# Banded attention: weights applied to the normalized rows first, value matrices a batch at a time

## The reference

```python
xq = _rms_norm(x @ wq, q_norm_w, EPS); xk = _rms_norm(x @ wk, k_norm_w, EPS); xv = x @ wv   # 8 heads of 128
bias = slopes[:, None, None] * rel             # rel = key position - query position
invalid = (rel > 0) | (rel < -WINDOW)          # a query sees itself and the 16 tokens before it
bias = jnp.where(invalid[None, :, :], NEG, bias)
probs = jax.nn.softmax(einsum('bhqd,bhkd->bhqk', q, k) * scale + bias[None], axis=-1)
y = einsum('bhqk,bhkd->bhqd', probs, v)        # then heads side by side
return y @ wo
```

## Time and profile before

| | us |
|---|---|
| runs, median of 3 | 1302.38 (1298.53 to 1306.37) |
| profiled execution | 1303.17 |
| its span | 1301.3 |
| banded attention on TensorE, first dM to last out1 | 972.17 to 1139.81 |
| TensorE busy, share of the span | 89% |
| VectorE | 70% |
| ScalarE | 67% |
| GpSimd | 48% |

### The profile page before, as it was taken

The page is one execution under the profiler, slowest core; times in us unless marked ns, Lnnn a source line. Parts: engine busy times, 40 slices in busy tenths (PEclk is TensorE's granted clock), DMA queues, the critical chain, the costliest instruction groups (busy, mean ns, idle before and its releaser), DMA issues.

```text
span 1301.3 us, 17124 instructions
## 1 busy us (share of the span) xinstructions
PE 1161.3 (89%) x6126; PEld 614.8 (47%) x6126; DVE 914.4 (70%) x1753; ACT 876.4 (67%) x1130; POOL 618.7 (48%) x455
## 2 busy tenths in 40 slices
PE   5899999999999999987888888999989999976865
PEld 2444444444444444422222222677766777733444
DVE  5666667766776677568989896255547777678885
ACT  2799999999989998963777777445545665633411
POOL 3577777777767776884555551033320000044232
PEclk8999999999999999986999999899999999978778
DMA  7100000000000000100000000000010000000000
GB/s 188 50 1 1 1 1 1 1 1 1 1 0 1 1 1 1 65 1 17 2 1 1 2 1 2 1 1 1 1 61 1 1 1 1 1 1 1 0 9 25
DMA packets 25631, 14.48 MB, mean 11 GB/s; under 512 B 14558, under 2 KB 24396, under 8 KB 25420
## 3 DMA queue, kind: packets, MB, share of 16 engines
q1 hardware_dynamic: 25548, 13.39, 3.7%
HBM read 12.34 MB, written 1.05 MB: 10 GB/s over the span
## 4 chain that ended last, share of the span: by engine, by line
PE 36%; POOL 30%; issue 19%; DVE 13%; ACT 1%; POOLq 0%; DMA 0%; SPq 0%; ACTq 0%; DVEq 0%
DVE ARENA L1048 6%; POOL ARENA L2466 6%; POOL ARENA L2464 6%; POOL ARENA L2460 6%; PE PS L914 4%; PE PS L889 4%; POOL WQ L2477 3%; POOL ARENA L2490 3%; PE PS L803 3%; PE PS L1269 3%; PE PS L1258 2%; PE PS L1253 2%; PE PS L1245 2%; PE PS L770 2%; PE PS L754 2%
## 5 line engine op out<-in xcount | busy, mean ns | idle before, releaser
L2320 DVE TENSOR_SCALAR ARENA<-PS,ARENA 128x512 f32<-128x512 f32 x256 | 174.6, 744 | 67.8 <-PE PS L1954 67.3
L1048 DVE TENSOR_REDUCE ARENA<-PS 128x1 f32<-128x512 f32 x256 | 161.1, 683 | 27.2 <-PE PS L770 26.6
L959 ACT ACTIVATE ARENA<-PS 128x1024 f32<-128x1024 f32 x128 | 128.8, 1026 | 58.3 <-PE PS L789 58.0
L2133 ACT ACTIVATE ARENA<-ARENA 128x2048 f32<-128x2048 f32 x64 | 122.2, 1911 | 62.3 <-DVE ARENA L2320 61.8
L1954 PE MATMUL PS<-ARENA 64*128 64x512 f32 x512 | 130.9, 631 | 0.0
L2140 ACT ACTIVATE ARENA<-ARENA,consts_sb 128x2048 f32<-128x2048 f32 x64 | 124.6, 1994 | 0.4
L1964 PE MATMUL PS<-ARENA 128*64 128x512 f32 x512 | 118.7, 606 | 1.3 <-issue 1.3
L2146 ACT ACTIVATE ARENA<-ARENA 128x2048 f32<-128x2048 f32 x64 | 118.3, 1897 | 0.0
L1204 POOL TENSOR_TENSOR ARENA<-ARENA 128x512 f32<-128x512 f32 x32 | 40.6, 1270 | 142.0 <-DVE ARENA L1162 141.9
L2473 POOL TENSOR_SCALAR WQ<-ARENA,consts_sb 128x512 bf16<-128x512 f32 x32 | 22.3, 695 | 159.8 <-DVE ARENA L2296 159.8
L770 PE MATMUL PS<-ARENA 32*128 32x512 bf16 x256 | 74.3, 405 | 25.7 <-DVE ARENA L1048 21.4
(11 more groups left out here) (279 smaller groups left out, 2693.6 us busy)
## 6 DMA issues: line engine op xcount, KB each, us to landing
ARENA<-in_window_bias_dram SPq DMA_DIRECT2D x1, 1536.0 KB, 6.8
WKVG<-in_L_attn_W_in_dram SPq DMA_DIRECT2D x3, 448.0 KB, 5.5
X<-in_x_dram SPq DMA_DIRECT2D x4, 256.0 KB, 4.4
W<-in_L_ffn_w_dram SPq DMA_DIRECT2D x1, 1024.0 KB
out_dram<-X SPq DMA_DIRECT2D x4, 256.0 KB, 2.3
BV<-in_L_attn_b_in_dram SPq DMA_DIRECT2D x1, 512.0 KB, 6.1
Wout<-in_L_attn_W_out_dram SPq DMA_DIRECT2D x1, 512.0 KB, 4.8
WQ<-in_L_attn_wq_dram SPq DMA_DIRECT2D x1, 512.0 KB, 3.3
```

Of the source, the lines that this page charges most:

```text
L959: act.activation(PT[m % PT_SLOTS], bank(("cP", m)), ACT.Exp, scale=0.5).then_inc(sem("c_exp"), 1)
L1048: dve.tensor_reduce(NMX[:, w % 2, t, h:h + 1], bank(("cS", n, j)), AX.X, ALU.max, negate=True).then_inc(sem("c_max"), 1)
L2133: act.activation(chunk(u, half), chunk(u, half), ACT.Sqrt).then_inc(sem("rooted"), 1)
L2320: dve.tensor_scalar(D[:, u % 2, kt, hd, :], bank(("S", u, c)), K2[:, u % 2, kt, hd:hd + 1], 1e-30, ALU.add, ALU.max).then_inc(sem("guarded ...
```

## The change

The product (band weights) x (rows) x (`NVO1` part) is made from the other side. The value matrices are gone. `finish(n)` now multiplies the tile's 128 keys as normalized rows, one stationary tile, with the turned weights of four heads at a time, two products of 4 x nq columns (dZ, two banks). ScalarE copies the first four heads' half and VectorE the second into `ZT`, which holds a batch. Only then, for a whole batch and in two parts (`project_out`: columns 0 to 351 once tile 2 is done, 352 to 511 once tile 4 is done), each head's part of `NVO1` is multiplied with its `ZT` columns and summed over the heads in dO. The key rows of tiles 0 and 4 lie in `Y` as they are; those of tiles 1 to 3 are turned back from `XT` once per batch (`turn_keys`, dX, three transposes) and copied by ScalarE to `KTOK`. VectorE's copy of the values goes. Out1 and the addition to the stream come one step later, and the turned next layernorm comes behind dT.

```diff
@@ -344,8 +344,19 @@
 
 def turned_out_batch(n):
 
-    b, ti = divmod(n - 1, len(TILES1))
+    b, ti = divmod(n - 2, len(TILES1))
     return b - 1 if ti == 0 and 1 <= b < B else None
+
+
+PARTS1 = ((0, 352, 3), (352, 512, 5))
+
+
+def projected(n):
+
+    b, ti = divmod(n, len(TILES1))
+    if ti == 4:
+        return b, 0
+    return (b - 1, 1) if ti == 1 and b else None
 
 
 def stage_d_jobs():
...
@@ -361,11 +372,11 @@
                 out += [(("dM", b, h), 1, [(("d_q", "d_k")[h % 2], HD1 // 2 * b + h // 2 + 1)], "D")]
             if b + 1 < B:
                 out += [(("yt", b + 1, m), 1, [("xqk", 2 * (b + 1) + m + 1)], "D") for m in range(2)]
-        return out + [(("dS", n), 2, [("d_biased", n + 1)], "D"), (("dV", n), 2, [("d_v", n + 1)], "D")]
+            out += [(("dX", b), 1, [("d_keys", b + 1)], "DO")]
+        return out + [(("dS", n), 2, [("d_biased", n + 1)], "D")]
 
     def finish(n):
-        b, ti = divmod(n, len(TILES1))
-        return [(("dO", b), 1, [("d_ot", b + 1)], "DO")] if ti == 0 else []
+        return [(("dZ", n), 2, [("d_z_low", n + 1), ("d_z_high", n + 1)], "D")]
 
     def turn_out(b):
         return [(("out1", b), 1, [("x_new", 3 * B + b + 1)], "D")]
...
@@ -374,13 +385,15 @@
     for n in range(steps):
         if n + 2 < steps:
             jobs += start(n + 2)
+        if projected(n) is not None and projected(n)[1] == 0:
+            jobs += [(("dO", projected(n)[0]), 1, [("d_ot", projected(n)[0] + 1)], "DO")]
         if turned_out_batch(n) is not None:
             jobs += turn_out(turned_out_batch(n))
         if n:
             jobs += finish(n - 1)
+        jobs += [(("dT", n), 2, [("d_pt", n + 1)], "D")]
         if n >= 9 and (n - 4) % len(TILES1) == 0:
             jobs += ln_job(4, n // len(TILES1) - 1, "D")
-        jobs += [(("dT", n), 2, [("d_pt", n + 1)], "D")]
     return jobs + finish(steps - 1) + turn_out(B - 1)
 
 
...
@@ -649,7 +662,9 @@
         WD = Wout[:, 0:3, :]
         QT1, at = carve(0, [HD1, S])
         OT1, at = carve(at, [S])
-        V1, at = carve(at, [4, HD1 * P])
+        KTOK, _ = carve(at, [2, 3, P])
+        at += 4 * HD1 * P
+        ZT, _ = carve(20480, [2, HD1, S])
         SM, at = carve(at, [3, HD1, P])
         PT1, at = carve(at, [2, HD1, P])
         XQK, at = carve(at, [2, 2, S])
...
@@ -702,8 +717,8 @@
         HQT, at = carve(at, [2, 2, 3 * P])
 
         for name in ("d_weights_in", "bias_in", "e_weights_in", "gram_turned", "gram", "zy", "ss", "r_log",
-                     "r_rms", "ym", "xqk", "d_q", "d_k", "d_biased", "d_v", "d_max", "d_exp", "d_norm", "d_pt",
-                     "d_ot", "d_summed", "folded_weights", "folded_values", "folded_scores", "e_k", "e_v4", "e_vx", "e_kx", "e_ctx4", "e_q", "e_biased", "e_shift", "e_max",
+                     "r_rms", "ym", "xqk", "d_q", "d_k", "d_biased", "d_keys", "d_z_low", "d_z_high", "d_max", "d_exp", "d_norm", "d_pt",
+                     "d_ot", "folded_weights", "folded_values", "folded_scores", "e_k", "e_v4", "e_vx", "e_kx", "e_ctx4", "e_q", "e_biased", "e_shift", "e_max",
                      "f_rounded", "f_added", "e_exp", "e_rc", "e_p", "e_pt", "e_o", "xb4", "mask_bias",
                      "f_weights_in", "f_wq", "f_w", "f_yq", "f_x", "f_silu", "f_h", "f_hq", "f_ht", "x_final"):
             sem(name)
...
@@ -1211,7 +1226,7 @@
 
         def turn_next(n):
 
-            return stats_next(n - 3)
+            return stats_next(n - 2)
         SCALE1 = float(P ** -0.5)
 
         def norms(pe, begin, done, b):
...
@@ -1232,6 +1247,14 @@
                     for t in range(QT):
                         mm = pe.transpose(o[:, t * P:(t + 1) * P], YM[:, m, t, :], ident)
                     done(mm, ("yt", b, m))
+
+            def turn_keys(b):
+                pe.wait_ge(sem("xt_ready"), norm_no(3, b))
+                o = begin(("dX", b))
+                for i in range(3):
+                    k0 = TILES1[i + 1][2]
+                    mm = pe.transpose(o[:, i * P:(i + 1) * P], XT[:, b, k0:k0 + P], ident)
+                done(mm, ("dX", b))
 
             def start(n):
                 b, ti = divmod(n, len(TILES1))
...
@@ -1246,6 +1269,7 @@
                              ("dM", b, h))
                     if b + 1 < B:
                         turn_y(b + 1)
+                    turn_keys(b)
                     pe.wait_ge(sem("d_q"), HD1 // 2 * (b + 1))
                     pe.wait_ge(sem("d_k"), HD1 // 2 * (b + 1))
                 o = begin(("dS", n)).rearrange("p k (h c) -> p (k h) c", c=P)
...
@@ -1253,25 +1277,31 @@
                     mm = pe.matmul(o[0:nq, h, :], QT1[:, h, q0:q0 + nq], XQK[:, b % 2, 1, k0:k0 + P],
                                    start=True, stop=True)
                 done(mm, ("dS", n))
-                o = begin(("dV", n))
+
+            def finish(n):
+
+                b, ti = divmod(n, len(TILES1))
+                nq = TILES1[ti][1]
+                pe.wait_ge(sem("d_pt"), n + 1)
+                pe.wait_ge(sem("d_keys"), b + 1)
+                keys = Y[:, b, 0, :] if ti == 0 else Y[:, b, QT - 1, :] if ti == 4 else KTOK[:, b % 2, ti - 1, :]
+                o = begin(("dZ", n))
                 for half in range(2):
-                    mm = pe.matmul(o[:, half, :], XT[:, b, k0:k0 + P], NVO1[:, half * 512:(half + 1) * 512],
-                                   start=True, stop=True)
-                done(mm, ("dV", n))
-
-            def finish(n):
-                b, ti = divmod(n, len(TILES1))
-                q0, nq, k0, _ = TILES1[ti]
-                pe.wait_ge(sem("d_pt"), n + 1)
-                pe.wait_ge(sem("d_v"), n + 1)
-                o = begin(("dO", b)) if ti == 0 else bank(("dO", b))
+                    mm = pe.matmul(o[:, half, 0:4 * nq].rearrange("p (h q) -> p h q", h=4), keys,
+                                   PT1[:, n % 2, 4 * half:4 * half + 4, 0:nq], start=True, stop=True)
+                done(mm, ("dZ", n))
+
+            def project_out(b, part):
+
+                q0, q1, tiles = PARTS1[part]
+                for name in ("d_z_low", "d_z_high"):
+                    pe.wait_ge(sem(name), len(TILES1) * b + tiles)
+                o = begin(("dO", b)) if part == 0 else bank(("dO", b))
                 for h in range(HD1):
-                    mm = pe.matmul(o[:, q0:q0 + nq], V1[:, n % 4, h * P:(h + 1) * P], PT1[:, n % 2, h, 0:nq],
-                                   start=ti == 0 and h == 0, stop=ti == len(TILES1) - 1 and h == HD1 - 1)
-                if ti == len(TILES1) - 1:
+                    mm = pe.matmul(o[:, q0:q1], NVO1[:, h * P:(h + 1) * P], ZT[:, b % 2, h, q0:q1],
+                                   start=part == 0 and h == 0, stop=part == 1 and h == HD1 - 1)
+                if part == 1:
                     done(mm, ("dO", b))
-                else:
-                    mm.then_inc(sem("d_summed"), 1)
 
             def turn_out(b):
                 pe.wait_ge(sem("d_ot"), b + 1)
...
@@ -1288,19 +1318,22 @@
             for n in range(STEPS1):
                 if n + 2 < STEPS1:
                     start(n + 2)
+                if projected(n) is not None:
+                    project_out(*projected(n))
                 if turned_out_batch(n) is not None:
                     turn_out(turned_out_batch(n))
                 if n:
                     finish(n - 1)
-                if turn_next(n) is not None:
-                    ln_turn(4, turn_next(n))
                 nq = TILES1[n % len(TILES1)][1]
                 pe.wait_ge(sem("d_norm"), n + 1)
                 o = begin(("dT", n)).rearrange("p k (h c) -> p (k h) c", c=P)
                 for h in range(HD1):
                     mm = pe.transpose(o[:, h, 0:nq], SM[0:nq, n % 3, h, :], ident[0:nq, 0:nq])
                 done(mm, ("dT", n))
+                if turn_next(n) is not None:
+                    ln_turn(4, turn_next(n))
             finish(STEPS1 - 1)
+            project_out(B - 1, 1)
             turn_out(B - 1)
 
         def rms(act, b):
...
@@ -1327,6 +1360,18 @@
                         act.copy(QT1[:, h], bank(("dM", b, h))).then_inc(sem("d_k"), 1)
                     if b + 1 < B:
                         turn_y(b + 1)
+                    full(act, ("dX", b))
+                    act.copy(KTOK[:, b % 2].rearrange("p t d -> p (t d)"), bank(("dX", b))[:, 0:3 * P]
+                             ).then_inc(sem("d_keys"), 1)
+
+            def z_out(n):
+                b, ti = divmod(n, len(TILES1))
+                q0, nq = TILES1[ti][0:2]
+                full(act, ("dZ", n))
+                if b >= 2:
+                    full(act, ("dO", b - 2))
+                act.copy(ZT[:, b % 2, 0:4, q0:q0 + nq], bank(("dZ", n))[:, 0, 0:4 * nq].rearrange("p (h q) -> p h q", h=4)
+                         ).then_inc(sem("d_z_low"), 1)
 
             def softmax(n):
                 nq = TILES1[n % len(TILES1)][1]
...
@@ -1362,11 +1407,14 @@
                     start(n + 2)
                 if n + 1 < STEPS1:
```

(47 more changed lines are left out.)

## The result

The changed kernel takes 1295.52 us (median of 20 runs, 1291.19 to 1300.61); the kernel before takes 1302.38 us (median of 20, 1298.23 to 1306.37). The ratio is 0.995, with a 95% interval of 0.9938 to 0.9962: 6.9 us, just beyond half a per cent. The forecast was 1297 in a range of 1290 to 1303.

A forecast was written before the change was run, and what follows sets the result against it. TensorE was taken to bound the kernel. Gains of 6.3 us at the start, 4.4 and 3.3 in the batches, less 8.2 at the end, net 5.8 (5.7 taken), gave 1297 us from 1302.38; range 1290 to 1303.

The forecast's parts named there:

- TensorE's price list: Per batch of five tiles: 17.62 us of products go, 14.14 come, so 39.24 becomes 35.76 us, 3.48 less.
- rival 4: dZ's four-head columns with steps between run slower than contiguous ones: at 10%, 0.7 us a batch; chance 0.21 with rival 2.
- Rival 2: Hand-offs cost 0.3 us more in each of 20 tiles, eating 5 us: 1301 to 1303; chance 0.21 with rival 4.
- Rival 1: The saving stays: addition in time, end costs only 2 to 4 us more: 1290 to 1293; chance 0.19.
- The wait for the addition: Next batch's first dM waits 1.05 us for VectorE's addition to the stream to free a bank, in two batches.
- The middle batches: From the second batch's dM to the fourth's: 36.8 us per batch, 73.6 together, a gain of 4.4.
- The start: Up to the second batch's dM: norm products begin 1.39 us earlier, and that dM comes 6.3 us earlier.
- The end: From the end of dT(17) to the last out1: 19.4 us, 8.2 longer than the 11.2 before.
- Rival 3: TensorE falls to the 1.2 GHz level in the end's gaps, adding up to 12.9 us: 1309.6; chance 0.08.
- a granted clock under 0.9 before the last addition: A sign, at the stage's end, that would show the forecast wrong.
- the zero for the clock: Nothing charged for a fall of TensorE's clock, despite end gaps of some 1.1, 1.0 and 1.9 us.
- who comes next after TensorE: In a plain tile ScalarE needs 4.4 to 4.5 us, VectorE 4.3 and TensorE 4.1; hand-offs pace such tiles.

The follow-up runs named there:

- e5: The changed kernel with the projection made in five parts per batch, one per tile, instead of two: 1301.63 us, 0.9992 of the kernel before.
- e3: The changed kernel with the old value products made again in each tile, read by nobody: 1328.82 us, 1.0204 of the kernel before.
- e1: The changed kernel with out1 in the two banks of dO instead of the six that rotate: 1292.17 us, 0.9918 of the kernel before.
- e6: The changed kernel with four products of 512 columns filling the pause before dT(0): 1295.5 us, 0.9943 of the kernel before.
- e8: The kernel of e7 with the pause before dT(0) filled as in e6: 1290.74 us, 0.9912 of the kernel before.
- e10: The changed kernel run and profiled again, word for word, on another chip: 1291.79 us, 0.9936 of the kernel before.
- e2: The changed kernel with ScalarE's scale factors computed behind tile 19's exponentials and its half of dZ(17): 1294.42 us, 0.9941 of the kernel before.
- e9: The changed kernel with one 128x1024-word operation (1.2 us) put on VectorE in each tile: 1313.53 us, 1.0086 of the kernel before.
- e12: The changed kernel with one 128x1024-word copy put on ScalarE in each tile: 1298.21 us, 0.9955 of the kernel before.
- e7: The changed kernel with the edits of e1 and e2 and the last batch's projection in three parts: 1289.08 us, 0.9896 of the kernel before.
- e4: The changed kernel with two products of 512 columns filling the pause before the last batch's projection: 1296.06 us, 0.9949 of the kernel before.

## Why the forecast was right, step by step

**TensorE's price list** held: 1.50, 1.72, 0.65, 4.74, 2.18 and 0.33 us, from two rates and a floor; the batch without waits comes within 0.1 us of the 35.76. The fear that four heads' columns with steps between them run slower (rival 4) is refuted by the 1.50, and the floor is shown by e5. That TensorE paces the middle is shown by e3, one to one. Rival 2 (hand-offs of 0.3 us a tile) is refuted by the chain of a batch, where plain tiles are TensorE's alone and the middle came out 0.2 us under the forecast. Rival 1's mild end is refuted by D.

**The wait for the addition** was predicted at 1.05 us and measured at 0.91; e1 takes it away. The middle batches came out at 73.42 for a forecast of 73.6.

**The start** was predicted 6.3 us shorter, and the work in it is (e6, e8). dT(0) came 1.55 us earlier in e10, counted from the first dM, for a forecast of 1.39, and from there to dM it takes 9.5 us for a forecast of 9.4 while the clock holds. The value products that filled the time before dT(0) were also what kept the clock up, as e6 shows by filling it with others; without them it falls in most executions and takes 1.4 us back. I had charged nothing for it.

**The end** gives back 8.3 us at full clock (19.52 against 11.21), forecast 8.2, on the chain that was named, as e2 shows. In after's profile the clock takes 1.5 more. Here my reading was too mild: I held that pauses of one to two microseconds were harmless, from windows where 2.10 of 3.10 us and 1.56 of 5.00 were busy, yet after 2.8 us of work in 6.2 it fell in three profiles of five. Rival 3 happened in small, at 1.5 us and not 12.9. I had named a granted clock under 0.9 before the last addition as a sign that I was wrong, and it came: 0.50. The term that was wrong is the zero for the clock, here and at the start.

The Trainium skill has a rule of clock swings from frequent waits as banks rotate (TensorE: Matmul & The Clock Gate, section "A second HAM failure mode: psum-queue depth-cycling"). In the changed kernel the two waits of 0.9 us at a bank leave the clock at 1.00, but two are few. In e9, where such a wait is 2.05 us, the clock fell behind one of the two. So the rule is not refuted here.

**Luck.** After's profile gives 161.72 us for the stage beside the forecast's 161.8, and part of that is chance: its first dM was 1.3 us shorter than the 9.96 of before, which made up for most of the 1.5 us that the clock took at the end, and the clock held at dT(0), as in two profiles of ten. In e10 neither was so, and the stage is 164.24, 3.4 us under before and not 5.9. With the clock up in both places and the first dM as long as before's it would be 161.5, as in e6. The median of 6.9 us lies above all of these; what the rest of the program adds to it is not shown.

**The step that was wrong without harm** is who comes next after TensorE. I gave ScalarE 4.4 to 4.5 us per plain tile and VectorE 4.3, and saw the risk in ScalarE (rival 2). e9 and e12 show the opposite order of risk: a microsecond on ScalarE in each tile costs 0.9 us in two batches, 1.14 on VectorE costs 6.5. VectorE carries the addition and half of each dZ just ahead of TensorE's need. So the relief of VectorE, which had no term of its own in my sum, was a condition of the gain: with an operation of the old copy's size put back, the kernel is slower than before.

**Why so little of so much.** By the price list TensorE's work fell by 3.48 us in each of four batches, 13.9 together. The middle kept 8.2 of it over three batches (78.03 + 39.40 to 73.42 + 35.79), and with 4.9 (e10) to 7.5 (after) at the start the lead was 13 to 16 us at dT(17). The end took 8 to 10 of it back: work that had been spread over the tiles now stands behind the last of them. e7 shows what was left to win: 3.4 us at the end and 1.8 at the wait in the middle.

## To carry to other kernels

Price a product by the larger of its moving columns and the floor that comes with a fresh stationary tile (0.108 us an instruction here). Gathering columns behind one stationary tile pays until the gathered work stands alone at the end of a stage, so gather in the middle and split at the end. When the busiest engine is relieved, measure the room of the next ones by loading each for a trial: their busy shares (27.92 and 26.66 us of 37.00 here) don't tell which one is late. Work that looks removable may be filling a pause in which the clock would fall. Compare the stretches of two profiles at the same granted clock before reading a difference of a microsecond or two.

## Not expected of the hardware

The granted clock at the same place of the same kernel differs between executions: behind the open pause before dT(0) it was 1.00 in two profiles and low in eight, behind one and the same wait of 2.05 us in e9 it fell once and stayed up once, and the last projection took 5.00 us or 6.40 to 6.69 in the kernels with the end as in after (8.02 in e9, where the granted clock over the 7.3 us ahead of it was 0.72 already). Filling one pause at the end moved the fall to the next piece (e4: 4.99, then 3.90 where 2.43 is the full-clock time).
